# Softmax on eight cores: one wide Exp per row block, normalise on ScalarE, layer norm sums in bf16

## The chip, the cores and the metric

The kernel runs on all 8 NeuronCores of one Trainium2 chip. Each core computes two of the sixteen sequences, with no exchange between cores. The metric is device time in microseconds of the slowest core; lower is better.

## What is computed

The reference is two transformer layers with the layer norm behind each part, on 16 sequences of 2,048 tokens and width 2,048. Cut to what matters:

```python
# layer 0: 32 heads of 64, causal, with a forget gate
logf = log_sigmoid(x @ Wf.T + bf); c = cumsum(logf)
scores = q @ k.T * scale + c[i] - c[j]
p = softmax(where(causal, scores, -inf)); attn = p @ v
x = layernorm(x + attn @ Wo.T)
x = layernorm(x + relu(x @ w_fc)**2 @ w_proj)      # ternary weights
# layer 1: 16 heads of 128, causal, biases
x = layernorm(x + attention(x))
x = layernorm(x + (silu(x @ w_gate * s) * (x @ w_up * s)) @ w_down * s)   # int8 weights
```

## The kernel before

A `Plan` holds all instructions in the order in which the code emits them, with the semaphore values that each waits for; `emit` writes each engine's share in that order. So every engine works strictly in program order. On every engine but TensorE, each instruction also waits for the one before it on that engine to be complete. A `fence` between stages makes every engine wait for all the others. `cx.used(key, engine)` notes who used a buffer last, and `cx.use_wait(key)` makes the next user wait for that.

Activations lie transposed, width on partitions. A core does, for each layer, weight preparation, then for each of its two sequences attention with output projection and layer norm, then the feed-forward part with layer norm.

**Attention** (`emit_l0a_seq` and, alike, `emit_l1a_seq`). For each head (32 in the first layer, 16 in the second) the loops `ic`, `ti4` run over 16 row blocks of 128 queries, ti = 0 to 15; block ti has ji = 128 (ti + 1) keys. I call one block a step. Scores go to the PSUM tile ps_s, four banks of 512 f32 columns, nb = 1 to 4 of them in use. A step emits, in this order:

1. TensorE: per bank one score matmul (L1447 in the first layer, L1006 in the second) and, in the first layer only, a second one of two rows that adds the gate's terms (L1455). A bank is written again once ScalarE has read it (`psS`).
2. VectorE: causal mask on the last 128 columns (L1463, L1015), maximum of each bank (L1470, L1022), then the negated maximum of these (L1479, L1030).
3. ScalarE: for each bank one Exp with that maximum as bias (L1487, L1038), which writes bf16 to one of two buffers `pn` and the bank's sum to a column of `sums4`. The sum is written by a read of the accumulator, which the profile shows as an instruction of its own.
4. VectorE: sum of the bank sums (L1499, L1050), reciprocal (L1505, L1056), and `pn` times it (L1509, L1060).
5. `flush` of the step before, ti - 1: TensorE transposes its `pn` in 128x128 tiles, up to eight into ps_tp (L1386, L949), and VectorE copies these eight to `ptbuf` (L1398, L961); for steps with more than eight tiles a second group follows, which waits for the copy of the first. After every fourth step come the matmuls with V (L1411, L974) and ScalarE's copy of the result (L1421, L984).

So the transposes of step ti stand on TensorE behind the scores of step ti + 1, and VectorE's copies of step ti - 1 stand behind the normalise of step ti. Step 15 of a head is flushed right after step 14.

At the head of each head the first layer prepares the gate's rows with four VectorE instructions over 16 partitions and two DMAs.

**Layer norm** (`emit_ln_chunk`), for each chunk of 512 tokens, 4 chunks x 2 sequences x 4 norms = 32 times: ScalarE squares the sixteen 128x512 f32 tiles of `ych` to bf16 (L355); TensorE adds up the tiles over partitions with a column of ones, in f32 (L364), then the squares in bf16 (L371); VectorE, ScalarE and VectorE make mean and 1/std of one row (L379 to L396); TensorE spreads both over the partitions (L400, L403); VectorE applies them (L410, L413).

## Time and profile before

| | us |
|---|---|
| timed runs of the kernel before | 31,814.4 and 32,193.6, median 32,004.0 |
| the profiled execution | 32,204.6 |
| its span, first to last instruction, slowest core | 32,201.4 |
| spans of the eight cores | 31,759.8 to 32,201.4 |
| TensorE busy | 19,485.8 (61%) |
| VectorE busy | 8,718.0 (27%) |
| ScalarE busy | 4,847.6 (15%) |

Busy times are sums over stages of different kinds. The granted clock is the share of TensorE's full 2.4 GHz that it was given; 0.5 is the lower of its two levels. In timelines a line gives start and length, the engine, the source line, output and input; square brackets tell how long the engine was idle before and who ended that.

### The profile page before, as it was taken

The page shows a single profiled execution, that of the slowest core. Times are in us where ns is not written, and L with a number is a line of the kernel's source. Part 1 is how long each engine was busy: PE and PEld are TensorE (multiplying, and loading weights), DVE is VectorE, ACT ScalarE, POOL GpSimd, SP SyncE. Part 2 cuts the span into 40 slices and gives each one's busy share as a digit, 9 for nine tenths or more (in the row PEclk, how much of TensorE's full clock was granted, in tenths as well). Part 3 has the DMA queues.
Part 4 walks back from the last instruction along what each step waited for, and adds up shares of the span by engine and source line. Part 5 has one row for each costly group of instructions (what it writes and reads, how often), then busy time and mean ns, then how long its engine had stood idle before and what let it go on. Part 6 is the DMA issues. An engine that isn't in the chain of part 4 may idle for free.

```text
span 32201.4 us, 233853 instructions; the slowest of 8 cores (31759.8 to 32201.4 us)
## 1 busy us (share of the span) xinstructions
PE 19485.8 (61%) x79002; PEld 8131.7 (25%) x79002; DVE 8718.0 (27%) x16972; ACT 4847.6 (15%) x10722; POOL 1507.5 (5%) x2577
## 2 busy tenths in 40 slices
PE   4745545684455461788636336933500888878888
PEld 2311111231111121333212112311200333333333
DVE  1144444204444436110211442044311000110001
ACT  2122222112222211202001220122100000000000
POOL 0000000000000000101000000000011000000000
PEclk9855555775555565889867556855655987788987
DMA  4100000310000036263541004100344112531144
GB/s 158 56 7 6 7 7 7 121 59 7 7 7 7 7 95 237 99 167 112 164 141 48 9 8 120 47 21 9 82 111 120 45 42 66 146 112 43 49 128 137
DMA packets 1209794, 2270.02 MB, mean 70 GB/s; under 512 B 626023, under 2 KB 734264, under 8 KB 1147096
## 3 DMA queue, kind: packets, MB, share of 16 engines
q1 hardware_dynamic: 1034426, 1692.00, 17.9%
q0 software_dynamic: 174208, 563.06, 5.3%
q8 instruction: 665, 10.90, 0.1%
q14 instruction: 495, 4.06, 0.0%
HBM read 1691.79 MB, written 562.90 MB: 70 GB/s over the span
## 4 chain that ended last, share of the span: by engine, by line
PE 55%; DVE 15%; DMA 13%; ACT 11%; issue 5%; SPq 1%; ACTq 0%; POOL 0%; DVEq 0%; POOLq 0%
PE ps_s L698 7%; PE ps_s L639 6%; PE ps_s L646 6%; ACT A L1487 5%; PE ps_s L459 4%; PE ps_s L1455 3%; PE ps_s L1447 3%; PE ps_s L508 3%; PE ps_s L857 3%; PE ps_s L1261 3%; ACT A L1038 3%; PE ps_z L1411 3%; DVE A L1470 2%; DMA wguT_s<-A 2%; PE ps_tp L1386 2%
## 5 line engine op out<-in xcount | busy, mean ns | idle before, releaser
L1386 PE MATMUL ps_tp<-A 128*128 128x128 bf16 x8704 | 1151.1, 299 | 2516.3 <-DVE A L1398 2495.5
L639 PE MATMUL ps_s<-A 128*128 128x512 bf16 x8192 | 2058.1, 410 | 668.2 <-ACT A L653 507.0
L1487 ACT ACTIVATE A<-ps_s,A 128x512 bf16<-128x512 f32 (+3 forms) x2560 | 1595.9, 623 | 4922.5 <-DVE A L1479 4872.6
L698 PE MATMUL ps_s<-A 128*128 128x512 bf16 x8192 | 2098.1, 428 | 299.1 <-DMA A<-wdT_s 299.1
L646 PE MATMUL ps_s<-A 128*128 128x512 bf16 x8192 | 2052.5, 409 | 0.0
L1470 DVE TENSOR_REDUCE A<-ps_s 128x1 f32<-128x512 f32 (+3 forms) x2560 | 1565.4, 611 | 1279.0 <-PE ps_s L1455 1215.2
L1447 PE MATMUL ps_s<-A 64*128 64x512 bf16 (+3 forms) x2560 | 1314.1, 513 | 856.6 <-ACT A L1487 784.8
L949 PE MATMUL ps_tp<-A 128*128 128x128 bf16 x4352 | 571.8, 296 | 1647.9 <-DVE A L961 1632.9
L1455 PE MATMUL ps_s<-A 2*128 2x512 bf16 (+3 forms) x2560 | 1323.8, 517 | 393.6 <-DMA A<-cs_sp 393.6
L1386 PEld LDWEIGHTS ps_tp<-A 128*128 128x128 bf16 x8704 | 787.4, 132 | 2925.7 <-issue 2893.7
L660 DVE SCALAR_TENSOR_TENSOR A<-ps_s,A 128x512 bf16<-128x512 f32 x512 | 384.5, 751 | 4153.4 <-ACT A L653 4153.4
L1411 PE MATMUL ps_z<-A 128*64 128x512 bf16 (+3 forms) x2560 | 919.5, 539 | 669.8 <-DVE A L1398 669.8
L508 PE MATMUL ps_s<-A 128*128 128x512 bf16 x5120 | 1139.0, 386 | 267.3 <-DMA A<-wprT_s 220.6
L639 PEld LDWEIGHTS ps_s<-A 128*128 128x128 bf16 x8192 | 808.8, 103 | 1918.2 <-issue 1515.6
L698 PEld LDWEIGHTS ps_s<-A 128*128 128x128 bf16 x8192 | 877.8, 107 | 1525.4 <-issue 1356.1
L459 PE MATMUL ps_s<-A 128*128 128x512 bf16 x5120 | 1147.0, 389 | 165.1 <-DMA A<-wfcT_s 99.6
L857 PE MATMUL ps_s<-A 128*128 128x512 bf16 x4096 | 984.7, 409 | 299.1 <-DMA A<-wk_s 296.7
L355 ACT ACTIVATE A<-A 128x512 bf16<-128x512 f32 x512 | 322.3, 629 | 5531.6 <-DVE A L712 2448.3
L646 PEld LDWEIGHTS ps_s<-A 128*128 128x128 bf16 x8192 | 848.1, 104 | 1117.9 <-issue 650.8
L1038 ACT ACTIVATE A<-ps_s,A 128x512 bf16<-128x512 f32 (+3 forms) x1280 | 797.9, 623 | 1927.7 <-DVE A L1030 1902.7
L1398 DVE COPY A<-ps_tp 128x1024 bf16<-128x1024 bf16 (+7 forms) x1536 | 823.4, 536 | 571.4 <-PE ps_tp L1386 538.2
L653 ACT ACTIVATE A<-ps_s,A 128x512 bf16<-128x512 f32 x512 | 352.0, 687 | 4158.4 <-PE ps_s L646 4158.3
(153 smaller groups left out, 19737.0 us busy)
## 6 DMA issues: line engine op xcount, KB each, us to landing
A<-wdT_s SPq DMA_DIRECT2D x512, 512.0 KB, 4.2
A<-wprT_s SPq DMA_DIRECT2D x512, 320.0 KB, 3.2
A<-wo_s SPq DMA_DIRECT2D x256, 512.0 KB, 5.5
A<-wguT_s SPq DMA_DIRECT2D x128, 1024.0 KB, 5.0
A<-L_ffn_w_fc SPq DMA_DIRECT2D x80, 1024.0 KB, 5.4
A<-L_ffn_w_proj SPq DMA_DIRECT2D x32, 2560.0 KB, 10.1
A<-r_b SPq DMA_DIRECT2D x256, 256.0 KB, 3.8
wguT_s<-A POOLq DMA_DIRECT2D x128, 512.0 KB, 4.8
```

Source lines behind the costliest of these rows:

```text
L459: pl.op("tensor", lambda e, pp=pp, wb=wb, db=db, tc=tc: e.matmul(out=pp, lhsT=wb[:, db * 128:(db + 1) * 128], rhs=xb[:, db * 2048 + tc * 5 ...
L508: pl.op("tensor", lambda e, pp=pp, wb=wb, co=co, hb=hb: e.matmul(out=pp, lhsT=wb[:, co:co + 128], rhs=hq[:, hb * 512:(hb + 1) * 512], star ...
L639: pl.op("tensor", lambda e, pp=ppg, b=gub, db=db, tc=tc: e.matmul(out=pp, lhsT=b[:, db * 128:(db + 1) * 128], rhs=xb[:, db * 2048 + tc * 5 ...
L646: pl.op("tensor", lambda e, pp=ppu, b=gub, db=db, tc=tc: e.matmul(out=pp, lhsT=b[:, 2048 + db * 128:2048 + (db + 1) * 128], rhs=xb[:, db * ...
L698: pl.op("tensor", lambda e, pp=pp, b=b, co=co, hb=hb: e.matmul(out=pp, lhsT=b[:, co:co + 128], rhs=fuseq[:, hb * 512:(hb + 1) * 512], star ...
L857: pl.op("tensor", lambda e, pp=pp, wb=wb, db=db, tc=tc: e.matmul(out=pp, lhsT=wb[:, db * 128:(db + 1) * 128], rhs=xb[:, db * 2048 + tc * 5 ...
L1386: pl.op("tensor", lambda e, pn=pn, tj=tj, half=half: e.transpose(out=ps["ps_tp"][:, half * 128:(half + 1) * 128], in_=pn[:, tj * 128:(tj + ...
L1411: pl.op("tensor", lambda e, tj=tj, o=o, h=h, ic=ic: e.matmul(out=ps["ps_z"][0:64, o:512], lhsT=v_sb[:, tj * 2048 + h * 64: tj * 2048 + h * ...
L1447: e.matmul(out=ps["ps_s"][:, jc * 512:jc * 512 + n], lhsT=qh[:, ti * 128:(ti + 1) * 128], rhs=kT[(h % 2) * 64:(h % 2) * 64 + 64, (h // 2) ...
L1455: pl.op("tensor", lambda e, jc=jc, n=n, ar=ar: e.matmul(out=ps["ps_s"][:, jc * 512:jc * 512 + n], lhsT=ones2, rhs=ar[0:2, jc * 512:jc * 51 ...
L1470: e.tensor_reduce(out=pmax[:, jc:jc + 1], in_=ps["ps_s"][:, jc * 512:jc * 512 + n], axis=AX.X, op=ALU.max),
L1487: sums4=sums4: e.activation(out=pn[:, jc * 512:jc * 512 + n], in_=ps["ps_s"][:, jc * 512:jc * 512 + n], func=AF.Exp, bias=negm, accum_out= ...
```

## The change

Three edits, the first two in both attention functions:

- The Exp pieces of a step become one Exp over all ji columns of ps_s, up to four banks, whose accumulator gives the whole row sum; `sums4` and the VectorE sum go. All banks are now given back together, at its end.
- The multiplication of `pn` by the reciprocal becomes an Identity ACTIVATE on ScalarE with the reciprocal as its scale. Transposes wait for ScalarE in its place.
- In the layer norm VectorE casts each tile of `ych` to bf16 (two slots), and the column sums run in bf16 on the cast tile.

```diff
@@ emit_ln_chunk
+    ybf = cx.vw("A3", 47104, BF16, 1024)
...
     for dt_ in range(DT):
-        pl.op("tensor", lambda e, dt_=dt_: e.matmul(
-            out=ps["ps_z"][0:1, :], lhsT=ones_f,
-            rhs=ych[:, dt_ * 512:(dt_ + 1) * 512],
+        sl = dt_ % 2
+        pl.op("vector", lambda e, dt_=dt_, sl=sl: e.tensor_copy(
+            out=ybf[:, sl * 512:(sl + 1) * 512],
+            in_=ych[:, dt_ * 512:(dt_ + 1) * 512]),
+            waits=list(y_ready) + cx.use_wait(("lnybf", sl)), inc="ve")
+        yb_ve = pl.v("ve")
+        pl.op("tensor", lambda e, dt_=dt_, sl=sl: e.matmul(
+            out=ps["ps_z"][0:1, :], lhsT=onesb,
+            rhs=ybf[:, sl * 512:(sl + 1) * 512],
             start=(dt_ == 0), stop=(dt_ == DT - 1)),
-            waits=list(y_ready) + (cx.use_wait("ps_z") if dt_ == 0 else []),
+            waits=[("ve", yb_ve)] + (cx.use_wait("ps_z") if dt_ == 0 else []),
             inc="te")
+        cx.used(("lnybf", sl), "te")
@@ emit_l1a_seq, and the same in emit_l0a_seq
-                    waits=[("ve", pnorm_ve)] +
+                    waits=[pnorm_ve] +
                           (cx.use_wait("pstp") if half == 0 else []),
...
-                sums4 = a4(cx, "sums40") if par == 0 else a4(cx, "sums41")
-                for jc in range(nb):
-                    n = min(512, ji - jc * 512)
-                    pl.op("scalar", lambda e, pn=pn, jc=jc, n=n, negm=negm,
-                          sums4=sums4: e.activation(
-                        out=pn[:, jc * 512:jc * 512 + n],
-                        in_=ps["ps_s"][:, jc * 512:jc * 512 + n], func=AF.Exp,
-                        bias=negm, accum_out=sums4[:, jc:jc + 1]),
-                        waits=[("ve", mx_ve)] +
-                              (cx.use_wait(("pn", ti4 % 2)) +
-                               cx.use_wait(("sums4", par)) if jc == 0 else []),
-                        inc="se")
-                    cx.used(("psS", jc), "se")
+                pl.op("scalar", lambda e, pn=pn, ji=ji, negm=negm, sums=sums:
+                      e.activation(
+                    out=pn[:, 0:ji], in_=ps["ps_s"][:, 0:ji], func=AF.Exp,
+                    bias=negm, accum_out=sums),
+                    waits=[("ve", mx_ve)] + cx.use_wait(("pn", ti4 % 2)),
+                    inc="se")
                 e_se = pl.v("se")
                 cx.used(("negm", par), "se")
-                pl.op("vector", lambda e, sums=sums, sums4=sums4, nb=nb:
-                      e.tensor_reduce(out=sums, in_=sums4[:, 0:nb], axis=AX.X,
-                                      op=ALU.add),
-                      waits=[("se", e_se)] + cx.use_wait(("sums", par)),
-                      inc="ve")
-                cx.used(("sums4", par), "ve")
+                for jc in range((ji + 511) // 512):
+                    cx.used(("psS", jc), "se")
                 pl.op("vector", lambda e, recipc=recipc, sums=sums:
                       e.reciprocal(out=recipc, in_=sums),
-                      waits=cx.use_wait(("recip", par)), inc="ve")
+                      waits=[("se", e_se)] + cx.use_wait(("recip", par)),
+                      inc="ve")
                 cx.used(("sums", par), "ve")
-                pl.op("vector", lambda e, pn=pn, ji=ji, recipc=recipc:
-                      e.tensor_scalar(
-                    out=pn[:, 0:ji], in0=pn[:, 0:ji], scalar1=recipc,
-                    scalar2=None, op0=ALU.mult), inc="ve")
-                cx.used(("recip", par), "ve")
-                pnorm_ve = pl.v("ve")
+                rc_ve = pl.v("ve")
+                pl.op("scalar", lambda e, pn=pn, ji=ji, recipc=recipc:
+                      e.activation(
+                    out=pn[:, 0:ji], in_=pn[:, 0:ji], func=AF.Identity,
+                    scale=recipc), waits=[("ve", rc_ve)], inc="se")
+                cx.used(("recip", par), "se")
+                pnorm_ve = ("se", pl.v("se"))
```

VectorE, end of step 13 and step 14 of a first-layer head, before:

```order
L1398 COPY A<-ps_tp 128x8x128
L1398 COPY A<-ps_tp 128x5x128
L1470 TENSOR_REDUCE A<-ps_s 128x1 x3
L1463 TENSOR_TENSOR ps_s<-ps_s,A 128x128
L1470 TENSOR_REDUCE A<-ps_s 128x1
L1479 TENSOR_REDUCE A<-A 128x1
L1499 TENSOR_REDUCE A<-A 128x1
L1505 RECIPROCAL A<-A 128x1
L1509 TENSOR_SCALAR A<-A 128x1920
L1398 COPY A<-ps_tp 128x8x128
L1398 COPY A<-ps_tp 128x6x128
```

The same place after the change (L1395 is the copy, L1467 and L1476 the maxima, L1460 the mask, L1491 the reciprocal):

```order
L1395 COPY A<-ps_tp 128x8x128
L1395 COPY A<-ps_tp 128x5x128
L1467 TENSOR_REDUCE A<-ps_s 128x1 x3
L1460 TENSOR_TENSOR ps_s<-ps_s,A 128x128
L1467 TENSOR_REDUCE A<-ps_s 128x1
L1476 TENSOR_REDUCE A<-A 128x1
L1491 RECIPROCAL A<-A 128x1
L1395 COPY A<-ps_tp 128x8x128
L1395 COPY A<-ps_tp 128x6x128
```

The sum and the normalise are gone; the copies follow the reciprocal at once.

ScalarE, steps 13 to 15 of a first-layer head and the start of the next, before (L1487 is Exp, L1421 the copy of the product with V):

```order
L1487 ACTIVATE A<-ps_s,A 128x512 x3
L1487 ACTIVATE A<-ps_s,A 128x256
L1487 ACTIVATE A<-ps_s,A 128x512 x3
L1487 ACTIVATE A<-ps_s,A 128x384
L1487 ACTIVATE A<-ps_s,A 128x512 x4
L1421 ACTIVATE A<-ps_z 64x512
L1487 ACTIVATE A<-ps_s,A 128x128
```

After (L1481 is Exp, L1497 the normalise, L1418 the copy):

```order
L1481 ACTIVATE A<-ps_s,A 128x1792
L1497 ACTIVATE A<-A 128x1792
L1481 ACTIVATE A<-ps_s,A 128x1920
L1497 ACTIVATE A<-A 128x1920
L1481 ACTIVATE A<-ps_s,A 128x2048
L1497 ACTIVATE A<-A 128x2048
L1418 ACTIVATE A<-ps_z 64x512
L1481 ACTIVATE A<-ps_s,A 128x128
```

Each step has one Exp and, behind it on the same engine, one normalise of the same width.

VectorE at the first layer norm chunk after the change (L1538 adds the residual, L364 is the cast):

```order
L1538 TENSOR_TENSOR A<-ps_s,A 128x512 x16
L364 CAST A<-A 128x512 x16
L385 TENSOR_SCALAR A<-ps_z 1x512
L388 TENSOR_SCALAR A<-ps_x 1x512
L392 TENSOR_TENSOR A<-A 1x512
```

Before, nothing stood between the sixteen additions and the row's first instruction; the casts are new there.

## Rows read from the trace of the kernel before

**Rows 1.** The cores: span and mean granted clock.
```profile
core 1: 32201.4 us, clock 0.698
```

**Rows 2.** The page: the chain that ended last, by engine.
```profile
PE 55%; DVE 15%; DMA 13%; ACT 11%; issue 5%; SPq 1%; ACTq 0%; POOL 0%; DVEq 0%; POOLq 0%
```

**Rows 3.** Busy time in two stretches: PE, PEld, DVE, ACT, POOL; PEclk, DMA share, GB/s.
```profile
2400.00:3200.00 800.00, 401.93 (x1501) 155.93 (x1501) 373.57 (x869) 180.73 (x492) 18.84 (x36) 0.53 0.03 7
...
18400.00:19200.00 800.00, 297.91 (x1458) 152.34 (x1458) 383.66 (x946) 206.32 (x559) 14.02 (x26) 0.56 0.03 9
```

**Rows 4.** Timeline of step 14 of a first-layer head: start, length in us.
```profile
2016.78 0.69 ACT L1487 ACTIVATE A<-ps_s,A 128x512 bf16<-128x512 f32 x1 [8.16 <-DVE A L1479]
...
2019.99 0.16 DVE L1499 TENSOR_REDUCE A<-A 128x1 f32<-128x4 f32 x1 [3.36 <-ACT A L1487]
...
2020.38 0.72 DVE L1509 TENSOR_SCALAR A<-A 128x1920 bf16<-128x1920 bf16 x1
2021.13 0.69 DVE L1398 COPY A<-ps_tp 128x1024 bf16<-128x1024 bf16 x1
...
2021.97 0.80 PE L1386 MATMUL ps_tp<-A 128*128 128x128 bf16 x6 [5.56 <-DVE A L1398]
...
2022.70 0.60 PE L1447 MATMUL ps_s<-A 64*128 64x512 bf16 x1
...
2026.46 0.60 PE L1455 MATMUL ps_s<-A 2*128 2x512 bf16 x1
...
2028.54 0.69 ACT L1487 ACTIVATE A<-ps_s,A 128x512 bf16<-128x512 f32 x1 [8.65 <-DVE A L1479]
```

**Rows 5.** Timeline of the next head: step 0, the mask of step 3, the head after it.
```profile
2051.82 0.37 ACT L1487 ACTIVATE A<-ps_s,A 128x128 bf16<-128x128 f32 x1 [6.92 <-DVE A L1479]
...
2052.38 0.15 DVE L1499 TENSOR_REDUCE A<-A 128x1 f32<-128x1 f32 x1 [0.65 <-ACT A L1487]
...
2059.54 0.30 DVE L1463 TENSOR_TENSOR ps_s<-ps_s,A 128x128 f32<-128x128 f32 x1 [0.23 <-PE ps_s L1455]
...
2187.73 0.37 ACT L1487 ACTIVATE A<-ps_s,A 128x128 bf16<-128x128 f32 x1 [6.57 <-DVE A L1479]
```

**Rows 6.** Timeline of step 7 of that head.
```profile
2083.85 0.49 DVE L1509 TENSOR_SCALAR A<-A 128x1024 bf16<-128x1024 bf16 x1
...
2085.03 1.42 DVE L1470 TENSOR_REDUCE A<-ps_s 128x1 f32<-128x512 f32 x2
```

**Rows 7.** Groups by line and shape: count, busy, mean ns, idle before.
```profile
L1505 DVE RECIPROCAL A<-A 128x1 f32<-128x1 f32 x1024 | 168.0, 164 | 41.4 <-DVE A L1499 6.7
...
L1056 DVE RECIPROCAL A<-A 128x1 f32<-128x1 f32 x512 | 84.0, 164 | 17.7
...
L1509 DVE TENSOR_SCALAR A<-A 128x2048 bf16<-128x2048 bf16 x64 | 48.2, 753 | 2.3
```

**Rows 8.** Timeline of ScalarE, first Exp of two second-layer heads.
```profile
18005.45 0.37 ACT L1038 ACTIVATE A<-ps_s,A 128x128 bf16<-128x128 f32 x1 [0.32 <-DVE A L1030]
...
18125.25 0.37 ACT L1038 ACTIVATE A<-ps_s,A 128x128 bf16<-128x128 f32 x1 [0.32 <-DVE A L1030]
```

**Rows 9.** Timeline of ScalarE, start of the second sequence, first layer.
```profile
6319.77 1.96 ACT L1226 ACTIVATE A<-ps_s,A 32x2048 f32<-32x2048 f32 x1 [132.05 <-PE ps_s L1216]
...
6323.69 1.28 ACT L1233 ACT_TABLE_LOAD   x1
```

**Rows 10.** A layer norm chunk: timeline; a cast group; busy time as rows 3.
```profile
5930.02 13.89 PE L364 MATMUL ps_z<-A 128*1 128x512 f32 x32 [1.01 <-DVE A L1550]
5930.03 10.55 ACT L355 ACTIVATE A<-A 128x512 bf16<-128x512 f32 x16 [95.01 <-DVE A L1550]
...
5943.75 3.62 PE L371 MATMUL ps_x<-A 128*1 128x512 bf16 x16
...
L837 DVE CAST A<-A 128x512 bf16<-128x512 f32 x128 | 54.6, 427 | 210.5 <-DMA A<-r_b 210.5
...
5930.00:5944.00 14.00, 13.98 (x34) 2.82 (x35) 0.00 (x0) 10.07 (x16) 0.00 (x0) 1.00 0.48 150
```

More of the change, by code:

```diff
@@ L1512, in emit_l0a_seq @@
[L1512 to L1513 removed]
+                rc_ve = pl.v("ve")
+                pl.op("scalar", lambda e, pn=pn, ji=ji, recipc=recipc:
+                      e.activation(
+                    out=pn[:, 0:ji], in_=pn[:, 0:ji], func=AF.Identity,
+                    scale=recipc), waits=[("ve", rc_ve)], inc="se")
+                cx.used(("recip", par), "se")
+                pnorm_ve = ("se", pl.v("se"))
                 flush_l0()
```

40 lines of the change are left out of this document (11 added, 29 removed).

## The prediction

> **What bounds the kernel now.** I read the spans of the cores first [rows 1]: the slowest core takes 32,201 us and the profiled execution 32,205, so some 3 us lie around the span. The two timed runs were 31,814 and 32,194, median 32,004; the profiled execution is 201 us over that median. The chain by engine [rows 2] gives TensorE a good half, with VectorE, DMA and ScalarE behind: no engine is the bound throughout, and the stages must be read apart. In the two attention stages [rows 3] TensorE is busy 50% (first layer) and 37% (second) at a mean granted clock of 0.53 and 0.56, that is mostly the lower of its two levels, VectorE 47 to 48% and ScalarE 23 to 26%. All are half idle, so what ends there is a chain that runs through the engines in turn.
>
> The chain of one softmax row block ("step", ti) is seen in [rows 4], step 14 of a head of the first layer: four Exp pieces on ScalarE (2016.78 to 2019.9), then VectorE alone: sum of the pieces, reciprocal, normalise, copy of the first eight transposes of the step before; then TensorE's second group of transposes, its eight score matmuls, VectorE's masks and maxima, and the next Exp at 2028.54. The period is 11.76 us and nothing in it overlaps. In steps 9 to 15 TensorE's idle time in front of the second group of transposes is ended by VectorE's copy, which stands behind the normalise.
>
> **The steps and their number.** The reciprocal runs once a step: 1,024 times in the first layer and 512 in the second [rows 7], that is 64 and 32 heads of 16 steps (both sequences). A head takes 2187.73 - 2051.82 = 135.9 us in the first layer and 18125.25 - 18005.45 = 119.8 in the second [rows 5, 8].
>
> **Part 1: one Exp in place of up to four.** In step 14 the four pieces take 3.21 us from the first start to VectorE's next instruction (2016.78 to 2019.99) [rows 4]. The trace has an ACTIVATE that reads 2,048 f32 columns of ps_s with a pointer for its bias: 1.96 us [rows 9]. A piece of 512 takes 0.69 us [rows 4], one of 128 takes 0.37 [rows 5], hence 0.83 us per 1,000 columns and 0.26 fixed, which gives the same 1.96 at 2,048. After a lone piece of 128, VectorE starts 0.56 us after it began, 0.19 more than its length (the accumulator's read) [rows 5]. So a fused Exp of 1,920 costs 0.26 + 1.59 + 0.19 = 2.05 where 3.21 stood: 1.16 less for three pieces fewer, 0.385 each. Steps 0 to 3 have one piece already and gain nothing.
>
> **Part 2: the sum of the pieces goes.** Sum and reciprocal take 0.39 us together (2019.99 to 2020.38 [rows 4]); the sum, 0.16 long, is half of it with its gap: 0.19 a step.
>
> **Part 3: the normalise moves from VectorE to ScalarE.** On VectorE it takes 0.72 us at 1,920 columns [rows 4], 0.753 at 2,048 [rows 7] and 0.49 at 1,024 [rows 6], that is 0.22 plus 0.26 per 1,000, and 0.03 of gap. On ScalarE no such instruction (Identity from SBUF with a pointer for its scale) stands in the trace; between the Square from SBUF, 0.66 apiece at 512 [rows 10], and the Identity of 2,048 columns, 1.96 [rows 9], I take 0.29 plus 0.83 per 1,000, 2.0 us at 2,048. It starts some 0.1 after the reciprocal. What hides it: its only reader is TensorE's transposes of the same step, which are queued behind the next step's score matmuls. In step 14 these end 2027.06 - 2020.38 = 6.7 us after the reciprocal [rows 4]; with the normalise gone from between still 5.9, against 2.1. ScalarE's own next Exp comes later yet. The tightest place is the last step, where no scores follow: the transposes of step 15 come after a copy (0.69), seven transposes (0.9, by the 0.80 of six [rows 4]) and a copy of those (about 0.6) with their handovers, about 2.6 us after the reciprocal against 2.1. If that cover went, 96 heads would pay some tenths each.
>
> The Trainium skill speaks against this move: "ScalarE: Activation LUTs", section "Rules for kernel authors", wants multiplications on VectorE, which it puts at up to about three times faster in bf16. The trace agrees on the engines (0.753 against my 2.0). By that rule, taken as a verdict on the whole, the move is a loss; it would be one where the longer instruction is waited for, and that is the second rival below.
>
> **The sum per head, first layer.** Steps 9 to 15 are a pure chain, as is step 8 and step 4 (there the product with V waits for the copy), so Exp, sum and normalise all count. Step 8: 0.77 + 0.19 + 0.55 = 1.51; steps 9, 10, 11: 1.54, 1.58, 1.62; steps 12 to 15 (three pieces fewer): 2.03, 2.07, 2.10, 2.13; together 14.6. Step 4: 0.385 + 0.19 + 0.39 = 0.96. In steps 5 to 7 VectorE runs without a pause from the sum to the maxima (in step 7 [rows 6] the normalise begins at 2083.85, the copy fits between, and the maxima follow with no idle time) and the next scores start when the first Exp piece is done (0.81 us in). With one Exp they start only when all of it is done (1.1 to 1.3 us), and each bank of scores then takes 1.07 us (seven of eight matmuls from 2022.70 to 2026.46 [rows 4]), so TensorE is late next: by this the three steps keep 0.35, 0.3 and 0.4 of their nearly 1 us each. Steps 0 to 3 wait for TensorE before the mask already [rows 5] and keep nothing. Sum 16.6 us; times 64 heads 1,062 us.
>
> **Second layer.** Scores need one matmul a bank, not two, so TensorE is not late in steps 5 to 7: they keep 1.0, 1.05 and 1.1. Steps 4 and 8 to 15 as above, 1.0 and 14.6; steps 1 to 3 some 0.7 together, by the same comparison. Sum 19.4; times 32 heads 621 us.
>
> **Part 4: the column sums of the layer norm in bf16.** There are 32 such chunks. TensorE's sixteen f32 sums take 13.7 us (two passes each), while ScalarE's sixteen squares take 10.55 beside them; then sixteen bf16 sums of squares take 3.6 us at full clock, and are over 17.35 us after the start [rows 10]. After the change VectorE casts (0.427 us apiece at 512 columns [rows 10]) and two slots alternate with short matmuls, 0.5 to 0.6 us apiece or 8 to 9.5 in all. ScalarE's squares, 10.55, are then late next, and the sums of squares start 3.1 us sooner. But TensorE, solidly busy until now at clock 1.00, is then about half busy, and stretches in which it is half busy stood at 0.53 [rows 3]. At the lower level sixteen matmuls need 6.8 us in place of 3.6 and the gain is gone (17.5 against 17.35). So the bounds are 0 and 3.2 us a chunk, 0 and 100 us in all; nearest are the half busy stretches, with some recovery in the run: I take 1 us, 32 us in all.
>
> **The sum.** 1,062 + 621 + 32 = 1,715 us. Against the profiled execution that is 32,205 - 1,715 = 30,490, against the median 30,289. I forecast their middle, 30,390 us. Own range of this case: Exp and normalise a tenth off either way and the timed runs' scatter, 30,050 to 30,700.
>
> **Rivals.**
> Faster clock. With 10 to 20% less idle time TensorE could spend more of the attention at its higher level. For it: after each product with V the clock is up for a moment. Against it: in step 14 TensorE works without a pause from 2021.97 to past 2027 on transposes and scores, and those matmuls still take 0.60 us [rows 4]. Its price: VectorE's maxima (0.72 a bank: 1.42 and a gap for two [rows 6]) would pace the scores in place of 1.07, 0.35 on 25 banks a head in 64 heads, 560 us; with transposes and products with V some 1,100 in all: 29,300 us.
>
> The normalise is waited for after all. If the transposes end up right behind it, each step pays ScalarE's price in place of VectorE's: 0.07 + 0.57 per 1,000 columns, over 16 steps 11 us a head, which eats the 11.5 (first layer) or 12.3 us (second) of the other two parts: 64 x 0.5 + 32 x 1.3 + 32 = 105 us gained, 32,000 or so. Against it stands the cover of 5 us shown above.
>
> A wide Exp is not cheaper. If four banks in one instruction cost as much as four instructions, part 1 falls: 24 x 0.385 = 9.2 us on 96 heads, 890 us, leaving 31,280. Against it the 1.96 of [rows 9].
>
> Slower: tables. Exp and Identity now alternate on ScalarE 1,536 times. A switch of table took 1.28 us in front of an Exp that followed a Square root's set [rows 9]. If every step had one in front of its Exp it would lie on the chain: 1,536 x 1.28 = 1,970 us, more than the 1,715 gained, so 32,205 + 255 = 32,460; it decides from 1.12 us a step on. Against it: in [rows 9] an Identity ran just ahead of the switch under the other set, and only the Exp called for the load. The Trainium skill, same page, section "Table sets: the hidden batching unit", says that identity is in every set; the trace agrees as far as these rows go.
>
> **Chances.** Forecast 0.78; faster clock 0.08; normalise waited for 0.06; wide Exp no cheaper 0.05; tables 0.03. About 2% (640 us) is what a measurement of this kernel can tell from no change. Faster by more than that takes the forecast, the clock and some of the wide Exp: 0.88; within 2%: 0.10; slower 0.02. The range goes from 29,850, part of the way to the faster clock, to 30,950, part of the way to the dear Exp.
>
> **What would show it.** Right: one Exp of 1.96 to 2.0 us plus its read at 2,048 columns; step 14 at 9.6 to 9.8 us in place of 11.76; heads of about 119 and 100 us; normalises on ScalarE for which no transpose waits except within tenths; VectorE busy 0.8 ms less; no table loads between Exp and Identity; layer norm sums over in 14.2 to 17.6 us. Wrong: transposes whose idle time is ended by the ScalarE normalise; an attention clock well over 0.56; score matmuls that wait for the long Exp in steps 8 and later.

## The result, and the profile after

The changed kernel takes 30,443 us (median of 11 runs, 30,033 to 31,378) where the kernel before takes 32,263 (10 runs, 31,814 to 33,089). The ratio is 0.944, with a 95% interval of 0.937 to 0.951: faster, by some 1,820 us. Forecast were 30,390 us and 1,715 us less.

The page of the kernel after, first its cores, busy times and the chain by engine (they answer to [rows 1, 2]):

```profile
core 7: 30655.7 us, clock 0.697
```

```profile
PE 19549.3 (64%) x78490; PEld 8149.9 (27%) x78490; DVE 7923.9 (26%) x14412; ACT 5880.0 (19%) x7650; POOL 1505.5 (5%) x2577
...
PE 57%; DMA 14%; DVE 13%; ACT 10%; issue 4%; SPq 1%; POOL 0%; ACTq 0%; DVEq 0%; POOLq 0%
```

VectorE is busy 794 us less and ScalarE 1,032 more, yet the program is shorter: what left VectorE stood on the chain, and most of what came to ScalarE does not. The two attention stages, columns as in [rows 3]:

```profile
2400.00:3200.00 800.00, 454.14 (x1709) 176.23 (x1708) 356.55 (x778) 278.98 (x351) 20.89 (x40) 0.53 0.03 8
...
17000.00:17800.00 800.00, 361.05 (x1728) 182.55 (x1728) 377.52 (x895) 332.66 (x416) 17.25 (x32) 0.58 0.03 11
```

The clock of the attention stayed near the lower of its levels (0.53; 0.58 where 0.56 stood; over both whole stages 0.53 and 0.56 before, 0.54 and 0.58 after), and 800 us of the first layer now hold 1,709 matmuls in place of 1,501.

Step 14 of a first-layer head, which answers to [rows 4], and the tail of step 15 behind it (timeline: start, length, engine, line, output and input, idle time before and who ended it):

```profile
2172.23 1.86 ACT L1481 ACTIVATE A<-ps_s,A 128x1920 bf16<-128x1920 f32 x1 [5.10 <-DVE A L1476]
...
2174.28 0.16 DVE L1491 RECIPROCAL A<-A 128x1 f32<-128x1 f32 x1 [2.20 <-ACT A L1481]
2174.48 0.69 DVE L1395 COPY A<-ps_tp 128x1024 bf16<-128x1024 bf16 x1
2174.54 1.90 ACT L1497 ACTIVATE A<-A 128x1920 bf16<-128x1920 bf16 x1 [0.36 <-DVE A L1491]
...
2175.32 0.80 PE L1383 MATMUL ps_tp<-A 128*128 128x128 bf16 x6 [3.46 <-DVE A L1395]
...
2180.34 1.03 PE L1383 MATMUL ps_tp<-A 128*128 128x128 bf16 x8
...
2181.88 1.97 ACT L1481 ACTIVATE A<-ps_s,A 128x2048 bf16<-128x2048 f32 x1 [5.45 <-DVE A L1476]
...
2184.30 2.00 ACT L1497 ACTIVATE A<-A 128x2048 bf16<-128x2048 bf16 x1 [0.36 <-DVE A L1491]
...
2186.86 1.01 PE L1383 MATMUL ps_tp<-A 128*128 128x128 bf16 x8 [0.88 <-DVE A L1395]
```

One Exp, and 2.05 us after its start the reciprocal; the copy of the transposes follows it at once, and the second group of transposes starts 3.09 us after the Exp where 5.19 stood. The next Exp comes after 9.65 us (11.76 before). The normalise, 1.90 us, ends at 2176.44; the transposes of its own step come at 2180.34. In step 15, the tightest place, it ends at 2186.30, and the transposes wait for VectorE's copy until 2186.86: 0.56 us are left.

Its groups by shape (line, count, busy, mean ns, idle before), and the normalise's waits in the first layer and in the second:

```profile
L1497 ACT ACTIVATE A<-A 128x2048 bf16<-128x2048 bf16 x64 | 128.1, 2002 | 23.3 <-DVE A L1491 23.3
L1481 ACT ACTIVATE A<-ps_s,A 128x2048 bf16<-128x2048 f32 x64 | 125.9, 1967 | 349.0 <-DVE A L1476 349.0
```

```profile
L1497 ACT ACTIVATE A<-A x1024: 401/1202/2002, 1368.8 to 10506.1; 128x128 bf16<-128x128 bf16 x22, 128x896 bf16<-128x896 bf16 x22, 128x1664 bf16<-128x1664 bf16 x22, 128x384 bf16<-128x384 bf16 x21
...
  PE ps_tp L1383: 1.1, 3
...
L1057 ACT ACTIVATE A<-A x512: 401/1202/2002, 16412.8 to 21258.8; 128x128 bf16<-128x128 bf16 x11, 128x512 bf16<-128x512 bf16 x11, 128x896 bf16<-128x896 bf16 x11, 128x1280 bf16<-128x1280 bf16 x11
...
  PE ps_tp L955: 51.7, 102
```

Of the second layer's 102 waits, half a microsecond each, 96 stand in steps 0, 3 and 5 of the 32 heads. The table of steps below shows that these steps became shorter all the same, so the waits are not what ends them.

The layer norm chunk, which answers to [rows 10]:

```profile
5276.50 10.55 ACT L354 ACTIVATE A<-A 128x512 bf16<-128x512 f32 x16 [92.39 <-DVE A L1538]
5276.51 0.89 DVE L364 CAST A<-A 128x512 bf16<-128x512 f32 x2
...
5278.14 8.65 PE L369 MATMUL ps_z<-A 128*1 128x512 bf16 x14 [0.22 <-DVE A L364]
...
5287.19 6.01 PE L377 MATMUL ps_x<-A 128*1 128x512 bf16 x16 [0.41 <-ACT A L354]
```

The column sums now end before the squares; the sums of squares wait for ScalarE and start 10.69 us after the chunk began (13.72 before), but take 6.01 in place of 3.62.

From the traces I worked out how long each stage lasts on the slowest core: attention from the first score matmul to ScalarE's last copy of a product with V, both sequences together; a layer norm chunk from the first square to the end of the sums of squares, mean of 32. The time is the median of the kernel's runs. Medians are over all runs, while the ratios leave out those in which one half of the chip stood at a lower clock than the other, and since the kernel before took 33,367 us in such a run, its only one beside e5 to e8, those kernels have no ratio of their own.

```
kernel                     attention 1st   attention 2nd   chunk    median us
before                         8,721.3         3,846.6     19.25     32,263
after                          7,659.1         3,217.1     16.19     30,443
e1_norm_sums_only              8,714.1         3,832.2     16.30     32,287
e2_one_exp_only                8,084.3         3,499.6     19.13     31,352
e3_normalise_only              8,267.8         3,607.4     19.25     31,469
e4_normalise_twice             7,680.2         3,279.2     16.25     30,727
e5_squares_in_step             7,658.0         3,215.7     11.09     30,497
e6_copies_first                6,784.3         2,842.4     16.08     29,127
e7_before_copies_first         6,781.1         3,062.8     19.80     29,970
e8_pieces_copies_first         6,683.2         2,951.2     19.15     29,113
e9_joined                      6,563.8         2,740.8     11.09     28,406
```

First layer -1,062 us, second -630, layer norm -98: 1,790 in all. The spans of the profiled executions differ by 1,546 only, since everything outside attention and chunks took 244 us longer. I put that down to TensorE's clock in the dense stages, which the last section shows; no run isolates it. The medians of 10 and 11 runs differ by 1,820.

And the steps of a head: median time from the last maximum of a step to that of the next, in us, first layer (a) and second (b). The head is the sum of its sixteen steps.

```
step      0    1    2    3    4    5    6    7     8    9   10   11    12    13    14    15   head
before a 2.44 2.89 3.40 3.90 7.07 4.75 5.14 5.68 10.99 8.66 9.31 9.88 14.66 11.10 11.75 24.61 136.2
after  a 2.44 2.89 3.40 3.90 6.07 4.40 4.90 5.33  9.48 7.11 7.72 8.26 12.58  9.04  9.65 22.26 119.4
before b 2.28 2.81 3.20 3.74 6.40 4.75 5.14 5.68 10.05 7.62 8.03 8.61 14.44  9.72 10.36 17.00 119.8
after  b 2.02 2.47 2.87 3.37 5.40 3.80 4.09 4.58  8.53 6.08 6.45 6.99 12.49  7.66  8.12 15.65 100.6
```

### The profile page after: what moved, and what is told of

Read it like the earlier page. It is cut to its first block, busy times and chain, and to the rows that moved or that the text cites. A ratio compares the mean times of both kernels' runs of the same rounds, so it can differ in the third digit from the quotient of the medians.

```text
span 30655.7 us, 226913 instructions; the slowest of 8 cores (30184.6 to 30655.7 us)
## 1 busy us (share of the span) xinstructions
PE 19549.3 (64%) x78490; PEld 8149.9 (27%) x78490; DVE 7923.9 (26%) x14412; ACT 5880.0 (19%) x7650; POOL 1505.5 (5%) x2577
## 4 chain that ended last, share of the span: by engine, by line
PE 57%; DMA 14%; DVE 13%; ACT 10%; issue 4%; SPq 1%; POOL 0%; ACTq 0%; DVEq 0%; POOLq 0%
PE ps_s L704 7%; PE ps_s L645 7%; PE ps_s L652 7%; ACT A L1481 4%; PE ps_s L465 4%; PE ps_s L1452 3%; PE ps_s L1444 3%; PE ps_s L863 3%; PE ps_s L514 3%; PE ps_s L1258 3%; PE ps_z L1408 3%; DVE A L1467 2%; DMA wguT_s<-A 2%; ACT A L1041 2%; DVE A L1028 2%
## 5 line engine op out<-in xcount | busy, mean ns | idle before, releaser
L645 PE MATMUL ps_s<-A 128*128 128x512 bf16 x8192 | 2086.7, 414 | 663.7 <-ACT A L659 506.7
L704 PE MATMUL ps_s<-A 128*128 128x512 bf16 x8192 | 2161.3, 438 | 290.9 <-DMA A<-wdT_s 290.9
L652 PE MATMUL ps_s<-A 128*128 128x512 bf16 x8192 | 2087.3, 414 | 0.0
L1467 DVE TENSOR_REDUCE A<-ps_s 128x1 f32<-128x512 f32 (+3 forms) x2560 | 1565.5, 612 | 1435.2 <-PE ps_s L1452 1380.0
L1481 ACT ACTIVATE A<-ps_s,A 128x128 bf16<-128x128 f32 (+15 forms) x1024 | 1195.0, 1167 | 3459.1 <-DVE A L1476 3459.1
L514 PE MATMUL ps_s<-A 128*128 128x512 bf16 x5120 | 1140.3, 387 | 260.9 <-DMA A<-wprT_s 209.5
L1497 ACT ACTIVATE A<-A 128x128 bf16<-128x128 bf16 (+15 forms) x1024 | 1230.3, 1202 | 372.8 <-DVE A L1491 372.2
L863 PE MATMUL ps_s<-A 128*128 128x512 bf16 x4096 | 1062.6, 432 | 299.1 <-DMA A<-wk_s 299.1
L465 PE MATMUL ps_s<-A 128*128 128x512 bf16 x5120 | 1110.7, 380 | 159.7 <-DVE A L451 159.7
L1258 PE MATMUL ps_s<-A 128*128 128x512 bf16 x4096 | 984.3, 409 | 52.0 <-DMA A<-wk_s 51.8
```

Of the source, the lines that this page charges most:

```text
L465: pl.op("tensor", lambda e, pp=pp, wb=wb, db=db, tc=tc: e.matmul(out=pp, lhsT=wb[:, db * 128:(db + 1) * 128], rhs=xb[:, db * 2048 + tc * 5 ...
L514: pl.op("tensor", lambda e, pp=pp, wb=wb, co=co, hb=hb: e.matmul(out=pp, lhsT=wb[:, co:co + 128], rhs=hq[:, hb * 512:(hb + 1) * 512], star ...
L645: pl.op("tensor", lambda e, pp=ppg, b=gub, db=db, tc=tc: e.matmul(out=pp, lhsT=b[:, db * 128:(db + 1) * 128], rhs=xb[:, db * 2048 + tc * 5 ...
L652: pl.op("tensor", lambda e, pp=ppu, b=gub, db=db, tc=tc: e.matmul(out=pp, lhsT=b[:, 2048 + db * 128:2048 + (db + 1) * 128], rhs=xb[:, db * ...
L704: pl.op("tensor", lambda e, pp=pp, b=b, co=co, hb=hb: e.matmul(out=pp, lhsT=b[:, co:co + 128], rhs=fuseq[:, hb * 512:(hb + 1) * 512], star ...
L863: pl.op("tensor", lambda e, pp=pp, wb=wb, db=db, tc=tc: e.matmul(out=pp, lhsT=wb[:, db * 128:(db + 1) * 128], rhs=xb[:, db * 2048 + tc * 5 ...
```

## The experiments

My theory: the chain of a step lost the gaps between Exp pieces, the sum and the normalise, and the dear normalise on ScalarE is covered. The rivals: the normalise is waited for; a wide Exp is worth nothing; the gain comes from the layer norm or from the clock. The first four kernels take the change apart, e5 asks what is left in the layer norm chunk, e6 to e8 what the order of the copies is worth, and e9 joins the parts. Beside the first four the kernel before took 32,248 us; e5 to e8 are compared with one another and by their stages.

### e1: The layer norm part alone

The kernel before with `emit_ln_chunk` of the kernel after; attention is untouched.

```diff
-            out=ps["ps_z"][0:1, :], lhsT=ones_f,
-            rhs=ych[:, dt_ * 512:(dt_ + 1) * 512],
+            out=ps["ps_z"][0:1, :], lhsT=onesb,
+            rhs=ybf[:, sl * 512:(sl + 1) * 512],
```

> The kernel before with the bf16 column sums alone. Both traces so far: from the first square to the end of the sums of squares a chunk took 17.3 us where TensorE's granted clock was 1.00 and 21.2 where it was lower (mean 19.2 over 32 chunks), and 15.5 to 17.0 (mean 16.2) after the change. My theory: this part is worth 3.0 us a chunk, about 100 us, and the attention stages stay at about 4,360 us (first layer, each sequence, first score to last product with V) and 1,920 (second). Rival (the prediction's own size): 1 us a chunk, 32 us. Rival: the half idle TensorE lowers the clock of what follows, and the matmul stages behind the chunks get longer by more than is gained.

Measured: 32,287 us in two runs beside 32,248, so no difference that can be told. The chunk went from 19.25 to 16.30 us, 94 us over 32 chunks, three times my term of 32. Why three times: a group of the kernel before, all its column sums:

```profile
L364 PE MATMUL ps_z<-A 128*1 128x512 f32 x1024 | 493.7, 645 | 33.4 <-DVE A L1102 8.6 <-DVE A L712 8.6 <-DVE A L522 8.1
```

Each of the 512 sums has two passes, and a pass is recorded with 645 ns on average. In the first layer's first sequence, where [rows 10] were read, it is 592. Chunk by chunk, 16 of the 32 took about 17.3 us, at a granted clock of 1.00, and the others about 21.2, at 0.81: there the sums of squares start 16.8 us into the chunk in place of 13.7 and take 4.4 in place of 3.6. Against 17.3 the new chunk gains 1.1, what I had taken; against 21.2 it gains 5. I had taken one chunk for all of them.

### e2: One Exp alone

Against the kernel after, with `emit_ln_chunk` of the kernel before:

```diff
-                rc_ve = pl.v("ve")
-                pl.op("scalar", lambda e, pn=pn, ji=ji, recipc=recipc:
-                      e.activation(
-                    out=pn[:, 0:ji], in_=pn[:, 0:ji], func=AF.Identity,
-                    scale=recipc), waits=[("ve", rc_ve)], inc="se")
-                cx.used(("recip", par), "se")
-                pnorm_ve = ("se", pl.v("se"))
+                pl.op("vector", lambda e, pn=pn, ji=ji, recipc=recipc:
+                      e.tensor_scalar(
+                    out=pn[:, 0:ji], in0=pn[:, 0:ji], scalar1=recipc,
+                    scalar2=None, op0=ALU.mult), inc="ve")
+                cx.used(("recip", par), "ve")
+                pnorm_ve = ("ve", pl.v("ve"))
```

> The kernel before with one Exp per step and without the sum, the normalise still on VectorE, layer norm as before. Theory, by the steps of the prediction: 11.5 us a head in the first layer (the stage at 4,360 - 32 x 11.5 = 3,990 us) and 12 in the second (1,920 - 16 x 12 = 1,730). Rival: a wide Exp is no cheaper, only the sum counts, 0.19 a step: first layer about 4,280, second about 1,880. Rival: the late release of the banks eats the gain: no stage shorter than 4,200.

Measured: 31,352 us (3 runs, 30,910 to 31,694). Attention is 637 us shorter in the first layer and 347 in the second. The rival of the wide Exp that is worth nothing is out: step 14 takes 10.48 us for 11.75. A head lost 10.4 us in the first layer (136.2 to 125.8), where I had expected 11.5, and 10.8 in the second by its stage, where I had expected 12. In the first layer this is because steps 5 to 7 stand at 4.39, 4.91 and 5.33 here too, exactly as in the whole change: TensorE is late there as soon as the banks come back together, with or without the normalise. I had allowed for that in the prediction and forgot it in this expectation. In the second, steps 5 to 11 each gain 0.06 to 0.08 us less than their terms, and steps 12 and 15 about 0.3 less; why stays open.

### e3: The normalise on ScalarE alone

Against the kernel before; the Exp pieces, their sum and the layer norm stay.

```diff
-                pl.op("vector", lambda e, pn=pn, ji=ji, recipc=recipc:
-                      e.tensor_scalar(
...
+                pl.op("scalar", lambda e, pn=pn, ji=ji, recipc=recipc:
+                      e.activation(
+                    out=pn[:, 0:ji], in_=pn[:, 0:ji], func=AF.Identity,
+                    scale=recipc), waits=[("ve", rc_ve)], inc="se")
```

> The kernel before with the normalise on ScalarE alone; Exp in pieces, sum on VectorE, layer norm as before. Theory: what VectorE spent on it leaves the chain from step 4 on, 7.1 us a head in the first layer (stage at 4,130 us) and 7.9 in the second (1,790). Together with the run of one Exp that is 65 us more in the first layer than the whole change gave (531), because only with pieces do the scores of steps 5 to 7 start early. Rival: the longer instruction is waited for, and the stages come out at 4,360 + 32 x (11 - 7) = 4,500 or more.

Measured: 31,469 us, one run. Attention is 453 us shorter in the first layer and 239 in the second. With e2's 637 and 347 that is 1,090 and 586, where both together gave 1,062 and 630: the parts add up to 1,677 of 1,692 us. In the first layer they overlap: steps 5 to 7 gain 0.94 us in e2, 1.48 in e3 and no more than 0.94 with both, as both meet the same late TensorE. I had expected an overlap of 65 us a sequence, and it is 14. But the steps with a product with V, 8, 12 and 15, part from the sum of the two runs' gains by 0.57, 1.24 and 0.94 us a head, and not all the same way, so the size of the overlap is not shown.

### e4: A second pass over pn: is the normalise covered?

Against the kernel after; the second pass leaves `pn` as it is.

```diff
                     scale=recipc), waits=[("ve", rc_ve)], inc="se")
                 cx.used(("recip", par), "se")
+                pl.op("scalar", lambda e, pn=pn, ji=ji: e.activation(
+                    out=pn[:, 0:ji], in_=pn[:, 0:ji], func=AF.Identity), inc="se")
                 pnorm_ve = ("se", pl.v("se"))
```

> The changed kernel with a second Identity pass over the same columns (scale 1, the values stay), so that the normalise on ScalarE lasts about twice as long: 19 us more of ScalarE a head. Theory: all of it is covered except in step 15, whose transposes now start 0.56 us after its normalise ends; there 2.03 - 0.5 = 1.5 us a head are paid: first layer 3,829 + 50 = 3,880 us, second 1,609 + 25 = 1,635, total +150. Rival (the normalise is waited for in every step): 19 us a head, first layer 4,440, second 1,910, total +1,800.

Step 15 of a head; it answers to 2184.30 and 2186.86 of the timeline above:

```profile
2192.90 2.00 ACT L1499 ACTIVATE A<-A 128x2048 bf16<-128x2048 bf16 x1 [0.36 <-DVE A L1493]
...
2194.94 1.91 ACT L1503 ACTIVATE A<-A 128x2048 bf16<-128x2048 bf16 x1
...
2197.10 1.01 PE L1385 MATMUL ps_tp<-A 128*128 128x128 bf16 x8 [2.51 <-ACT A L1503]
```

```profile
L1503 ACT ACTIVATE A<-A x1024: 309/1110/1910, 1369.4 to 10387.6; 128x128 bf16<-128x128 bf16 x22, 128x896 bf16<-128x896 bf16 x22, 128x1664 bf16<-128x1664 bf16 x22, 128x384 bf16<-128x384 bf16 x21
...
  PE ps_tp L1385: 244.5, 315
```

Measured: 30,727 us (3 runs, 30,598 to 30,891). ScalarE has 1,536 passes more, by their mean of 1.11 us some 1,700 us, and attention grew by 21 us in the first layer and 62 in the second. I had expected 50 and 25 a sequence, 150 in all. Of the first layer's 315 waits 64 stand in step 15 and nearly all the others in steps 0, 3, 5 and 6, with 0.3 to 0.4 us each; those steps keep their length, so the second pass lengthens only the last step there: from 22.26 to 22.98 us. In the second layer the transposes wait for the second pass in nine of the sixteen steps, and again only step 15 shows it, from 15.65 to 17.15 us.

The second layer's 1.5 us are what I had expected. The first layer's 0.7 are less because the product with V at the end of step 15 took 5.06 us where 5.97 stood, at a mean granted clock of 0.65 against 0.55. Step 8 became 0.63 us shorter (9.48 to 8.85); its product with V takes 2.95 us in both kernels, but what follows it up to the next maximum ran at a mean of 0.92 against 0.68. So the rival "the normalise is waited for" falls. In the first layer the cover is as the prediction had it: deep in steps 4 to 14, half a microsecond in step 15. In the second it is thinner, as the 102 waits showed already, but what is waited for there ends no step.

### e5: Sums of squares in step with the squares

Against the kernel after: the second stream of sums goes into the loop of the first, each waiting for its own square.

```diff
         cx.used(("lnybf", sl), "te")
-    for dt_ in range(DT):
         pl.op("tensor", lambda e, dt_=dt_: e.matmul(
             out=ps["ps_x"][0:1, :], lhsT=onesb,
...
-            waits=[("se", casts_se)] + (cx.use_wait("ps_x") if dt_ == 0 else []),
+            waits=[("se", casts_se - (DT - 1 - dt_))] +
+                  (cx.use_wait("ps_x") if dt_ == 0 else []),
```

The same chunk as above, busy time of its eleven microseconds (columns as in [rows 3]), stands behind what was expected.

> The changed kernel; in the layer norm the sum of squares of each tile is now issued right behind the column sum of the same tile, and not behind all sixteen. Theory: ScalarE's squares (10.55 us) are then the only bound and the sums end at about 11.2 us in place of 16.2, 5 us a chunk, 160 us in all, whatever the clock, since each matmul waits for its square. Rival: the stretch of half idle TensorE costs the matmuls behind it as much; then the total does not move though the chunk is shorter.

```profile
5278.00:5289.00 11.00, 9.50 (x32) 2.53 (x32) 6.66 (x17) 9.86 (x16) 0.00 (x0) 1.00 0.55 187
```

Measured: the chunk takes 11.09 us (11.07 to 11.12 over all 32), which is ScalarE's 10.55 and one matmul. With two matmuls per tile TensorE is busy 9.50 of these 11 us and its clock is 1.00 in the chunk shown: the thing I feared in part 4, a half idle TensorE, goes away with it. Over the 32 chunks the clock is 0.72 to 1.00, where it was 0.56 to 0.90 in the kernel after. The total, 30,497 in one run beside 30,443, does not show the 163 us. Over the 24 intervals from chunk to chunk within a stage, the mean of the cores fell by 83 us where 24 x 5.1 = 122 were due; cores differ by 100 among themselves, so what became of the rest isn't settled.

### e6: The copies ahead of the reciprocal

In the changed kernel VectorE idles through the Exp (2.20 us in front of L1491 above), and the copy that TensorE waits for stands right behind. So I moved `flush` ahead of the reciprocal.

```diff
                 for jc in range((ji + 511) // 512):
                     cx.used(("psS", jc), "se")
+                flush_l0()
                 pl.op("vector", lambda e, recipc=recipc, sums=sums:
                       e.reciprocal(out=recipc, in_=sums),
...
-                flush_l0()
                 pending[0] = (pn, ti, pnorm_ve)
```

> The changed kernel with the flush of the step before (transposes, copies, products with V) emitted ahead of the reciprocal, so that VectorE's copies run beside the Exp. Theory: what is late next after the change is reciprocal, copy and second transposes between the end of the Exp and the next scores (1.9 us in step 14, from 2174.18 to 2176.05); with them under the Exp, step 14 goes from 9.65 to 7.9 us, a head loses 12.9 us in the first layer and about 14 in the second: stages of 3,415 and 1,380 us, total about -1,280. Rival: the normalise, now later, is no longer covered, and steps 9 to 14 gain less than 0.5 us each.

Step 14 of a first-layer head:

```profile
2497.37 0.69 DVE L1395 COPY A<-ps_tp 128x1024 bf16<-128x1024 bf16 x1
2497.48 1.86 ACT L1481 ACTIVATE A<-ps_s,A 128x1920 bf16<-128x1920 f32 x1 [3.31 <-DVE A L1476]
...
2499.58 0.58 PE L1444 MATMUL ps_s<-A 64*128 64x512 bf16 x1 [0.58 <-ACT A L1481]
2499.70 0.16 DVE L1492 RECIPROCAL A<-A 128x1 f32<-128x1 f32 x1
2499.96 1.90 ACT L1498 ACTIVATE A<-A 128x1920 bf16<-128x1920 bf16 x1 [0.53 <-DVE A L1492]
...
2505.39 1.97 ACT L1481 ACTIVATE A<-ps_s,A 128x2048 bf16<-128x2048 f32 x1 [3.54 <-DVE A L1476]
```

Measured: 29,127 us, 1,370 less than e5 beside it, although its layer norm chunks are 160 us longer in all; attention is 1,247 us shorter. The other 283 us lie outside both, where e5's slowest core spent 8.3 ms at a clock of 0.81 and e6's 6.2. A sequence takes 3,392 us in the first layer and 1,421 in the second, where 3,415 and 1,380 were expected. The copies and the second transposes run under the Exp; what the scores wait for now is the Exp, and step 14 takes 7.91 us.

### e7: The same order in the kernel before

```diff
+                flush_l0()
                 pl.op("vector", lambda e, sums=sums, sums4=sums4, nb=nb:
                       e.tensor_reduce(out=sums, in_=sums4[:, 0:nb], axis=AX.X,
...
-                flush_l0()
                 pending[0] = (pn, ti, pnorm_ve)
```

> The kernel before with the flush emitted ahead of the sum; Exp in pieces, normalise on VectorE. It tells what part of the gain of the change could have been had by order alone. By the chain: the next scores start some 1.7 us after the Exp does, since the pieces give the banks back one by one, and step 14 goes from 11.75 to about 8.2 us; first layer about 3,460 us a sequence, second about 1,570: faster than the changed kernel in both. Rival: VectorE's normalise is still in front of the maxima and keeps the steps at 10 us or more.

```profile
2492.03 0.69 DVE L1398 COPY A<-ps_tp 128x1024 bf16<-128x1024 bf16 x1
2492.15 0.69 ACT L1487 ACTIVATE A<-ps_s,A 128x512 bf16<-128x512 f32 x1 [4.62 <-DVE A L1479]
...
2493.60 0.60 PE L1447 MATMUL ps_s<-A 64*128 64x512 bf16 x1
...
2495.35 0.16 DVE L1500 TENSOR_REDUCE A<-A 128x1 f32<-128x4 f32 x1 [1.02 <-ACT A L1487]
...
2495.74 0.72 DVE L1510 TENSOR_SCALAR A<-A 128x1920 bf16<-128x1920 bf16 x1
...
2500.04 0.69 ACT L1487 ACTIVATE A<-ps_s,A 128x512 bf16<-128x512 f32 x1 [4.79 <-DVE A L1479]
```

Measured: 29,970 us (3 runs, 29,906 to 30,239): the order alone, with the pieces, the sum and VectorE's normalise all kept, takes 2,724 us out of attention and beats the changed kernel. Here pieces are an advantage: the first bank is free 0.8 us into the Exp, the scores of the next step run beside the other pieces, and sum and normalise lie beside them too. Step 14 takes 7.89 us, as in e6. So in the first layer what the change removed was on the chain only because the copies stood behind it: attention there takes 6,781 us here and 6,784 in e6. In the second layer that does not hold, as e6 is shorter by another 220 us (2,842 against 3,063).

### e8: Pieces, copies first, normalise on ScalarE

The kernel of the last section with the edit of the third, in both layers:

```diff
+                flush_l0()
                 pl.op("vector", lambda e, sums=sums, sums4=sums4, nb=nb:
...
+                    out=pn[:, 0:ji], in_=pn[:, 0:ji], func=AF.Identity,
+                    scale=recipc), waits=[("ve", rc_ve)], inc="se")
```

> As the run before, with the normalise on ScalarE too (Exp still in pieces, layer norm as before). Theory: in the first layer, where TensorE needs 1.07 us a bank, the early release of the banks is worth more than the shorter Exp: step 14 at 7.6 us against 7.9 with one Exp, stage about 3,300 us. In the second layer, where VectorE's 0.72 us a bank paces, the pieces cost: step 14 at 7.4 against 6.4 with one Exp, stage 1,470 against 1,380. Rival: one Exp is better in both.

```
step      0    1    2    3    4    5    6    7     8    9   10   11    12    13    14    15   head
e6     a                     4.77 4.40 4.91 5.34  7.23 5.90 6.41 6.84  9.96  7.40  7.91 22.03 105.7
e8     a                     4.77 4.18 4.58 4.91  7.75 5.33 5.97 6.22 10.94  6.84  7.29 23.46 104.9
e6     b                     4.11 3.80 4.09 4.53  6.80 4.76 5.25 5.68 10.36  6.10  6.40 16.02  88.6
e8     b                     4.11 3.76 4.06 4.49  7.08 5.30 5.60 6.03  9.71  6.84  7.13 17.19  92.0
```

Measured: 29,113 us in two runs. Between e6 and e8 only the form of the Exp differs, with the sum that the pieces need (and the layer norm). In the first layer the pieces win 0.2 to 0.6 us in steps 5 to 7, 9 to 11, 13 and 14 and lose in steps 8, 12 and 15; in the second layer one Exp wins from step 8 on, but for step 12, and the head. The first layer's scores take two matmuls, 1.07 us a bank, so I had expected an early start to be worth more there than the gaps between pieces; the steps agree, but no run varies the matmuls alone. In step 15 no scores follow, and the pieces only cost.

### e9: A version from the parts

It is e6 with the layer norm of e5. In the first layer it uses the pieces and their sum where `pieces` holds (ti is 4 ic + ti4), and one Exp elsewhere; in both layers step 15 is normalised on VectorE.

```diff
+                pieces = ti4 != 0 and ti < 15 and nb > 1
+                if pieces:
...
+                if ti < 15:
+                    rc_ve = pl.v("ve")
...
+                else:
+                    pl.op("vector", lambda e, pn=pn, ji=ji, recipc=recipc:
+                          e.tensor_scalar(
```

> The changed kernel with: flush ahead of the reciprocal in both layers; in the first layer Exp in pieces again in the steps after step 4 that no product with V precedes (5 to 7, 9 to 11, 13, 14) and one Exp elsewhere, in the second layer one Exp throughout; the normalise of step 15 on VectorE in both; squares summed in step. Theory: step by step the shorter of what the runs of copies first and of pieces with copies first showed, step 15 another 1.1 us shorter since 0.78 us of VectorE replace 2.1 of ScalarE where nothing covers them: a head of 100.8 us in the first layer (105.7 with copies first) and 87.5 in the second (88.6), layer norm sums at 11.1 us. Total 29,127 - 314 - 35 - 160 = 28,620 us. Rival: mixing the forms moves waits elsewhere, and the heads stay at 105 and 88.

Step 15 of a first-layer head, where nothing covers the normalise:

```profile
2476.87 0.75 DVE L1540 TENSOR_SCALAR A<-A 128x2048 bf16<-128x2048 bf16 x1
...
2477.77 1.01 PE L1393 MATMUL ps_tp<-A 128*128 128x128 bf16 x8 [1.86 <-DVE A L1540]
```

Measured: 28,406 us (4 runs, 28,344 to 28,750); the ratio to the kernel before, beside it in 7 runs, is 0.883, 95% interval 0.872 to 0.894. Expected were 28,620 us. By their steps the heads take 102.2 and 85.2 us, where 100.8 and 87.5 were expected. Step 15 fell from e6's 22.03 to 20.79 us in the first layer and from 16.02 to 13.39 in the second. That is the place where VectorE's 0.75 us beat ScalarE's 2.00, as the transposes wait for it. In the first layer the 1.24 us are about the difference of the two instructions. Of the second layer's 2.63 us the product with V at the step's end has 1.22 (6.08 to 4.86 us, at a mean clock of 0.66 against 0.54), which the normalise's place does not explain.

Steps 8 and 12 of the first layer, to which I had given one Exp for their sake, stayed at 7.75 and 10.95, e8's values: their difference between e6 and e8 does not come from the form of that step's Exp. The traces show where it lies. In step 8 the product with V takes 2.95 us in all three, and what follows it 3.4, 3.7 and 3.9 us on average (e6, e8, e9), at clocks of 0.96, 0.71 and 0.53. In step 12 the product itself takes 3.89, 4.66 and 4.66 us, at 0.62, 0.51 and 0.50. What makes the clock rise sooner in one kernel than in another stays open.

## Why the prediction was right

**The chain.** By the steps of the tables: step 4 lost 1.00 us (0.96 predicted), step 8 1.51 (1.51), steps 9 to 11 1.55, 1.59 and 1.62 (1.54, 1.58, 1.62), steps 12 to 14 2.08, 2.06 and 2.10 (2.03, 2.07, 2.10), step 15 2.35 (2.13). Step 4's term left out the 0.03 us of gap behind the normalise, which the other steps have; with it, it is 0.99. Step 15's product with V took 5.97 us in place of 6.17, which is the 0.2 above the forecast. A period that is a pure chain changes by the sum of what is taken out, and these are the periods where each link ends the idle time of the next.

**What is late next.** Steps 5 to 7 of the first layer: 0.35, 0.24 and 0.35 us (0.35, 0.3, 0.4), against 0.95, 1.05 and 1.10 in the second (1.0, 1.05, 1.1). Head: 16.8 us (16.6) and 19.2 (19.4). In the second layer two misses cancel: steps 0 to 3 gave 1.30 us (0.7), step 15 1.35 (2.13). Step 15's 0.78 are its product with V, which took 5.62 us where 4.85 stood, at a mean clock of 0.59 against 0.63: the sum has no term for the clock of these products. Stages: 1,062 (1,062) and 630 (621). That the first agrees to the microsecond is luck, as a head lost 16.8 us and not 16.6, and as e2 and e3 add up to 28 us more than the two together gave.

**The total.** That 30,390 came so near to 30,443 is luck in part. The forecast starts from 32,105, between a profiled execution and the median of two runs, and the median of ten is 32,263: the start was 158 us too low and the gain 105 too small, and the two cancel but for 53.

**Sizes that the trace didn't show.** The wide Exp, put at 1.96 us from the 32-partition Identity of [rows 9], took 1.967; the Identity with a pointer scale from SBUF, put at 2.0, took 2.002. Its 0.29 us of fixed cost does not follow from the two rows named, through which a line has 0.23 and reaches 1.96; measured are 0.401 us at 128 columns and 2.002 at 2,048, which give the 0.29. From Exp to reciprocal step 14 took 2.05 us, as predicted.

**The cover.** 2.6 us against 2.1 were foreseen at step 15; 0.56 us were left. The Trainium skill's wish for VectorE ("ScalarE: Activation LUTs", "Rules for kernel authors") gave the price rightly, 2.00 against 0.75 us, and e4 shows that the price alone decides nothing: another 1,700 us of it cost 83. e9 shows where it does decide, in step 15, with 1.2 us a head in the first layer.

**Part 4 was mis-sized.** 32 us predicted, 98 measured in the stage. That is the edge of the 0 to 100 it gave as bounds. The step that failed is "TensorE's sixteen f32 sums take 13.7 us": read from one chunk at clock 1.00 and used for 32, of which half stood at a clock of 0.81, with 16.8 us and a chunk of 21.2. The fear beside it was half right: the sums of squares took 6.01 us in the chunk shown and 4.8 to 6.3 over all, mean 5.5, not the 3.6 of full clock and not the 6.8 of the lower.

**The rivals.** Faster clock: 0.53 and 0.58, no. Wide Exp not cheaper: e2, no. Normalise waited for: e3 and e4, no. Tables: the trace after has the same 12 table loads as before, none between an Exp and an Identity; the Trainium skill says that identity is in every set ("ScalarE: Activation LUTs", "Table sets: the hidden batching unit"), and the trace agrees. Not foreseen was the clock of the dense stages, beside which the profiled spans differ by 1,546 us only; that it is no effect of the change is argued, not shown.

## What to carry to other kernels

In a pipeline of half idle engines, add up the links that end each other's idle time, step by step, and ask of each step what is late next; busy times say nothing of it, and an instruction moved to an engine three times slower is free, or nearly so (83 us for 1,700 in e4), as long as its reader comes later. Before making the links shorter, look whether one of them could stand elsewhere: the copies put under the Exp were worth more than everything the change did, and in the first layer they changed which form of Exp is the better one. A price read from one instance of a stage is a price at that instance's clock.
